# Destination rows of the message stage by a second gather, in place of a load and a 0/1 matrix

## What is computed

```python
m = x @ W_n2m.T                       # x: output of layer 0, normed
q, k, v = (m @ Wq.T + bq), (m @ Wk.T + bk), (m @ Wv.T + bv)
kj = k[src] + e                       # e from edge_attr
alpha = softmax over the edges of one dst of (q[dst] * kj).sum * scale
out = segment_sum((v[src] + e) * alpha, dst)
x_r = m @ Wskip.T + bskip
beta = sigmoid([out, x_r, out - x_r] @ Wbeta.T)
x = layernorm(x + (beta * x_r + (1 - beta) * out) @ W_m2n.T)
```

## Time and profile before

| | |
|---|---|
| median of 3 runs | 1339.7 us (1338.72 to 1341.64) |
| the profiled execution | 1339.14 us, its span 1337.4 us |
| Message, first gather to the second softmax's first transposes | 725.2 to 1107.4 us |
| steady part of it read below | 744.8 to 1080 us, 94 tiles |

### The profile page before, as it was taken

How to read it: one execution, slowest core, us unless ns; L and a number is a source line. 1 busy time by engine, 2 the same in 40 slices (tenths; PEclk the granted TensorE clock), 3 DMA queues, 4 the chain that set the end, 5 groups by cost and what they waited for, 6 DMA issues and landing times. The chain is left out here.

```text
span 1337.4 us, 29091 instructions
## 1 busy us (share of the span) xinstructions
PE 1190.2 (89%) x7386; PEld 1055.2 (79%) x7386; DVE 1042.9 (78%) x3852; ACT 813.8 (61%) x2583; POOL 839.6 (63%) x1060
## 2 busy tenths in 40 slices
PE   4999999999986899899996899999999995799990
PEld 3888999989974777777775799999999994687770
DVE  4667777777779788888885888888888877798870
ACT  1566666666657756566566566666666667376661
POOL 4888887888843645455454666666666643188885
PEclk9999999999998999999999899999999998799995
DMA  6778888888853678777786766766666632466641
GB/s 165 224 233 264 273 279 257 271 275 261 269 172 111 195 228 237 237 249 237 243 242 207 229 201 190 206 190 196 206 194 201 196 128 84 141 206 197 200 137 55
DMA packets 208940, 277.09 MB, mean 207 GB/s; under 512 B 40060, under 2 KB 140563, under 8 KB 208777
## 3 DMA queue, kind: packets, MB, share of 16 engines
q1 hardware_dynamic: 188793, 224.13, 54.3%
q0 software_dynamic: 19264, 50.85, 12.9%
q10 hardware_dynamic: 720, 0.26, 0.1%
HBM read 159.73 MB, written 117.12 MB: 207 GB/s over the span
## 5 line engine op out<-in xcount | busy, mean ns | idle before, releaser
L744 PE MATMUL banks<-m_ext,node_XT 128*128 128x257 f32 x1568 | 377.8, 384 | 0.0
L744 PEld LDWEIGHTS banks<-m_ext,node_XT 128*128 128x128 f32 x1568 | 286.6, 193 | 32.9
L671 POOL TENSOR_TENSOR node_r<-node_vv,half 128x4 f32<-128x4 f32 (+1 forms) x202 | 212.2, 1050 | 17.2 <-POOL node_vv L666 0.5
L770 DVE SCALAR_TENSOR_TENSOR node_X<-banks,node_be,node_X 128x256 f32<-128x256 f32 x392 | 169.7, 474 | 57.9 <-ACT node_be L696 56.2
L702 ACT ACTIVATE node_XT<-banks 128x512 f32<-128x512 f32 x196 | 117.1, 597 | 136.4 <-PE banks L734 129.5
L666 POOL TENSOR_SCALAR node_vv<-node_mv 128x4 f32<-128x4 f32 (+1 forms) x202 | 54.3, 269 | 202.7 <-DVE node_mv L778 182.8
L763 DVE BATCH_NORM_STATS2 node_st<-node_X 128x6 f32<-128x256 f32 x392 | 145.8, 413 | 18.5 <-DMA node_X<-in_x 17.2
L709 ACT ACTIVATE node_sq<-node_X 128x256 f32<-128x256 f32 x392 | 157.5, 406 | 0.0
L683 ACT ACTIVATE node_X<-node_X,node_r 128x256 f32<-128x256 f32 x326 | 146.0, 496 | 16.4 <-POOL node_r L671 16.4
L734 PE MATMUL banks<-ident,node_X 128*128 128x128 f32 x784 | 122.5, 279 | 29.3 <-DVE node_X L784 14.9
L824 POOL DMA_INDIRECT ring<-in_x,src_col x100 | 109.5, 1095 | 35.7 <-issue 13.8
(11 more groups left out here) (267 smaller groups left out, 2764.0 us busy)
## 6 DMA issues: line engine op xcount, KB each, us to landing
node_X<-in_x SPq DMA_DIRECT2D x196, 256.0 KB, 3.5
out<-node_X SPq DMA_DIRECT2D x196, 256.0 KB, 3.3
ring<-rows SPq DMA_DIRECT2D x210, 128.0 KB, 3.5
rows<-ring SPq DMA_DIRECT2D x100, 256.0 KB, 4.6
rows<-ring SPq DMA_DIRECT2D x200, 128.0 KB, 3.3
MB<-keeps SPq DMA_DIRECT2D x40, 320.0 KB, 5.3
store<-rows SPq DMA_DIRECT2D x90, 128.0 KB, 3.8
MB<-picks SPq DMA_DIRECT2D x50, 128.0 KB, 3.9
```

Source lines behind the costliest of these rows:

```text
L671: pool.tensor_tensor(r[:, s % 4, NT * lo:NT * hi], v, self.c.half[:, NT * lo:NT * hi], ALU.pow).then_inc(self.roots, 1)
L744: last = pe.matmul(ps[:, NT * o + k, 0:D + 1], self.XT[:, o, k * D + h * P:k * D + (h + 1) * P], c.m_ext[:, h, :], start=(h == 0), stop=(h ...
L770: last = dve.scalar_tensor_tensor(out=X[:, n % U, k, :], in0=ps[:, b + k, 0:D], scalar=self.be[:, n % 4, k:k + 1], in1=X[:, n % U, k, :], ...
```

## The change

In Message, side 0 of a ring slot is now fetched like side 1: by an indirect DMA on POOL, with the places `dst_pos` of the last edge of each edge's run. `dst_pos` comes out of the Positions part: the row of places is turned on PE and copied by ACT as integers to one column for each tile. Both sides are transposed on PE. The plain loads, the table and its loads, the comparison, the matrix product, and the gather and rewriting of the tails are gone. POOL now waits itself for the slot's earlier store (`kept`). The scratch tiles `inside` and `picked`, the tensors `tail_pos`, `lane` and `picks` are gone with them, and Output's semaphore counts are adapted.

```diff
@@ -493,23 +492,25 @@
-        self.own_sem, self.asks, self.answers, self.ready, self.table = (sem(n) for n in ("own_sem", "asks", "answers", "ready", "table"))
+        self.own_sem, self.asks, self.answers, self.ready, self.turned, self.columns = (sem(n) for n in ("own_sem", "asks", "answers", "ready", "turned", "columns"))
         def emit(s):
+            return
+        return emit
+
+    def pool(self, pool):
+        def emit(s):
+            return
+        return emit
+
+    def scalar(self, act):
+        c = self.c
+
+        def emit(s):
             if s == 3:
-                sp.wait_ge(self.ready, 1)
-                sp.dma_start(self.c.picks, self.c.scratch.picked).then_inc(self.table, 16)
-        return emit
-
-    def pool(self, pool):
-        def emit(s):
-            return
-        return emit
-
-    def scalar(self, act):
-        def emit(s):
-            return
+                act.wait_ge(self.turned, 1)
+                act.activation(c.dst_pos[:, :], c.psum[:, 7, 0:TILES], ACT.Copy).then_inc(self.columns, 1)
         return emit
...
@@ -526,6 +527,9 @@
                 pe.transpose(ps[0:TILES, 7, 256:256 + H], c.run2[:, 1, 1:TILES + 1], c.ident[0:H, 0:H]).then_inc(self.answers, 1)
+            if s == 3:
+                pe.wait_ge(self.ready, 1)
+                pe.transpose(ps[:, 7, 0:TILES], c.scratch.last, c.ident[0:TILES, 0:TILES]).then_inc(self.turned, 1)
         return emit
...
@@ -557,17 +561,13 @@
                 own(dve.tensor_copy(c.carried[:, 1, :], ps[0:TILES, 7, 256:256 + H]))
-                own(dve.memset(w.picked, -1.0))
-                own(dve.tensor_copy(c.lane[:, :], c.own_pos[:, 0:1]))
+                own(dve.memset(w.last, 1.0))
                 for k in range(2):
                 own.done()
-                own(dve.tensor_copy(c.tail_pos[:, :], w.top[:, EDGES - 1:EDGES]))
-                own(dve.tensor_scalar(w.inside, w.top, c.ends_of[:, EDGES:EDGES + 1], None, ALU.subtract))
-                own.done()
-                own(dve.scalar_tensor_tensor(out=w.picked[:, 1:1 + EDGES], in0=w.inside, scalar=float(P), in1=w.inside, op0=ALU.is_lt, op1=ALU.mult))
+                own(dve.tensor_copy(w.last[:, 1:1 + EDGES], w.top))
                 own.done()
...
@@ -874,8 +874,7 @@
                     act.wait_ge(self.masks.table, 16)
-                    act.wait_ge(self.positions.ready, 1)
-                    act.wait_ge(self.positions.table, 16)
+                    act.wait_ge(self.positions.columns, 1)
                 act.activation(c.store[:, n, 0:HP], ps[:, 6, 0:HP], ACT.Copy).then_inc(self.h_ready, 1)
...
@@ -940,6 +939,8 @@
                 n = s - 1
+                if n == 0:
+                    pe.wait_ge(self.positions.columns, 1)
                 pe.wait_ge(self.pointed, n + 1)
...
@@ -1272,12 +1270,8 @@
         self.r = sb("r", [P, 3, 4])
-        self.gathered, self.rows_in, self.kept = c.ring_in, c.ring_load, c.ring_out
-        self.in_before, self.rows_before, self.out_before = 32 * (TILES // c.R), 16 * (TILES // c.R), 32 * (TILES // c.R)
-        self.picks = [sem(f"picks{k}") for k in range(3)]
-        self.tails_in, self.tails_out, self.chosen = sem("tails_in"), sem("tails_out"), sem("chosen")
-        self.rows_v = c.rows[0:ROWS, :].rearrange("(t p) d -> t p d", p=P)
-        self.picks_v = c.picks.rearrange("(q k) m -> q (k m)", k=2)
+        self.gathered, self.kept = c.ring_in, c.ring_out
+        self.in_before, self.out_before = 32 * (TILES // c.R), 32 * (TILES // c.R)
         self.attrs = [sem(f"attrs{k}") for k in range(2)]
...
@@ -1301,12 +1295,12 @@
                     pool.wait_ge(self.finder.settled, 6)
-                    pool.wait_ge(self.positions.ready, 1)
-                    pool.indirect_dma_start(out=self.tails, out_offset=None, in_=c.rows,
-                                            in_offset=bass.IndirectOffsetOnAxis(ap=c.tail_pos[:, 0:1], axis=0)).then_inc(self.tails_in, 16)
+                    pool.wait_ge(self.positions.columns, 1)
                 at_least(pool, self.turned, n - R + 1)
-                pool.indirect_dma_start(out=c.ring[:, n % R, 1, :], out_offset=None, in_=c.rows,
-                                        in_offset=bass.IndirectOffsetOnAxis(ap=c.src_pos[:, n:n + 1], axis=0)).then_inc(self.gathered[n % R], 16)
+                pool.wait_ge(self.kept[n % R], self.out_before + 16 * (n // R))
+                for side, col in ((1, c.src_pos), (0, c.dst_pos)):
+                    pool.indirect_dma_start(out=c.ring[:, n % R, side, :], out_offset=None, in_=c.rows,
+                                            in_offset=bass.IndirectOffsetOnAxis(ap=col[:, n:n + 1], axis=0)).then_inc(self.gathered[n % R], 16)
             if t % 2 == 0 and live(t, -2, TILES):
...
@@ -1327,19 +1321,6 @@
                 sp.dma_start(self.into[n, :, :], c.ring[:, n % R, 0, :]).then_inc(self.kept[n % R], 16)
-            if live(t, -self.A, TILES):
-                n = t + self.A
-                if n == 0:
-                    sp.wait_ge(self.positions.table, 16)
-                    sp.wait_ge(self.tails_in, 16)
-                    sp.dma_start(self.rows_v[:, 0, :], self.tails).then_inc(self.tails_out, 16)
-                    sp.wait_ge(self.tails_out, 16)
-                sp.wait_ge(self.kept[n % R], self.out_before + 16 * (n // R))
-                sp.dma_start(c.ring[:, n % R, 0, :], self.rows_v[n, :, :]).then_inc(self.rows_in[n % R], 16)
-                if n % 2 == 0:
-                    at_least(sp, self.chosen, n - 4)
-                    sp.dma_start(self.picked[:, n // 2 % 3, :, :].rearrange("p k n -> p (k n)"),
-                                 self.picks_v[n // 2:n // 2 + 1, :].to_broadcast([P, 2 * P])).then_inc(self.picks[n // 2 % 3], 16)
             if t % B == 2 and live(t, -6, TILES):
...
@@ -1363,11 +1344,9 @@
                 at_least(pe, self.zt_ready, t)
-                pe.wait_ge(self.chosen, t + 1)
-                for h in range(2):
-                    pe.transpose(ps[:, 5, h * P:(h + 1) * P], c.ring[:, t % R, 1, h * P:(h + 1) * P], c.ident[:, :])
-                for h in range(2):
-                    last = pe.matmul(ps[:, 5, (2 + h) * P:(3 + h) * P], c.ring[:, t % R, 0, h * P:(h + 1) * P], self.pick[:, t % 4, :], start=True, stop=True)
+                for side in range(2):
+                    for h in range(2):
+                        last = pe.transpose(ps[:, 5, (2 * side + h) * P:(2 * side + h + 1) * P], c.ring[:, t % R, 1 - side, h * P:(h + 1) * P], c.ident[:, :])
                 last.then_inc(self.turned, 1)
...
@@ -1439,8 +1418,7 @@
                 n = t + 3
-                dve.wait_ge(self.gathered[n % R], self.in_before + 16 * (n // R + 1))
-                dve.wait_ge(self.rows_in[n % R], self.rows_before + 16 * (n // R + 1))
+                dve.wait_ge(self.gathered[n % R], self.in_before + 32 * (n // R + 1))
                 at_least(dve, self.measured, n - 1)
...
@@ -1458,11 +1436,6 @@
                 last.then_inc(self.measured, 1)
-            if live(t, -2, TILES):
-                n = t + 2
-                dve.wait_ge(self.picks[n // 2 % 3], 16 * (n // 6 + 1))
-                at_least(dve, self.turned, n - 3)
-                dve.tensor_scalar(self.pick[:, n % 4, :], self.picked[:, n // 2 % 3, n % 2, :], c.lane[:, 0:1], None, ALU.is_equal).then_inc(self.chosen, 1)
             if live(t, -1, TILES):
...
```

More of the change, by code:

```diff
@@ L152, in __init__ @@
         self.top = take(TILES, EDGES)
-        self.inside = take(TILES, EDGES)
-        self.picked = take(TILES, P)
+        self.last = take(TILES, P)
 LOADS = 16 * (1 + 4 + 6 + 3 + 1 + 3 + 5)
@@ L494, in sem @@
             return c.semaphore(nc, ctx, "positions_" + name)
-        self.own_sem, self.asks, self.answers, self.ready, self.table = (sem(n) for n in ("own_sem", "asks", "answers", "ready", "table"))
+        self.own_sem, self.asks, self.answers, self.ready, self.turned, self.columns = (sem(n) for n in ("own_sem", "asks", "answers", "ready", "turned", "columns"))
     def sync(self, sp):
         def emit(s):
-            if s == 3:
-                sp.wait_ge(self.ready, 1)
-                sp.dma_start(self.c.picks, self.c.scratch.picked).then_inc(self.table, 16)
+            return
         return emit
@@ L893, with __init__ @@
     FIRST, LAST = 0, TILES // 4 + 1
-    def __init__(self, nc, c, ctx, io):
-        self.c = c
+    def __init__(self, nc, c, ctx, io, positions):
+        self.c, self.positions = c, positions
         self.src = io["src"].rearrange("(s a e) -> s a e", a=1, e=self.B * EDGES)
@@ L1263, in __init__ @@
         self.attr_v = io["edge_attr_64"].rearrange("(q k e) a -> q e k a", k=self.B, e=EDGES)
-        self.picked = c.MB_flat[:, self.B * P:self.B * P + 6 * P].rearrange("p (a k n) -> p a k n", a=3, k=2)
-        self.pick = c.MSG_flat[:, 2 * self.B * RAD:2 * self.B * RAD + 4 * P].rearrange("p (a n) -> p a n", a=4)
-        self.tails = c.AT_flat[0:TILES, 0:D]
```

(8 more changed lines are left out.)

## The result

The changed kernel takes **1367.3 us** (median of 4 runs, 1366.2 to 1368.0); the kernel before, timed beside it, takes 1340.7 (1338.7 to 1342.7). The ratio is 1.0184, with a 95% interval from 1.0162 to 1.0206: slower. The profiled execution took 1368.0 us and its span is 1366.2, against 1339.1 and 1337.4 before.

What follows compares the result with a forecast made beforehand. PE bounds Message now at 3.57 us a tile; with the change POOL would at 3.85. The profiled 1339.1 us + 17.2 for the later softmax + 2 for waits = 1358; own range 1350 to 1366, outer 1338 to 1375.

Steps and rivals of the forecast that it cites:

- A further gather costs 1.25 us.: POOL in Message: each added gather occupies 1.25 us, gap included, raising POOL from 2.60 to 3.85 us a tile.
- The rival in which the gaps could be hidden: POOL in Message: gaps aren't work, so PE stays the bound; 1312 us, or about 1328; 9 in 100.
- PE, 0.24 us less a tile.: PE in Message: transposes replace products, saving 0.24 us a tile, to 3.32; the most the change could give.
- PE busy about 87%: Sign in the changed kernel's Message, about 745 to 1106 us: PE busy about 87% at full clock.
- 2 us for waits of POOL.: Message: allowance of 2 us in all for POOL waiting on DVE's statistics.
- The rival in which POOL waits as well: Message: gathers land late, so POOL's power waits too; up to 33 us more, 1366 to 1391; 12 in 100.
- The start.: Start of Message: six more gathers paid by a wait that goes; POOL's power at L1316 19.2 us after the first gather.
- The end, -8.9 us.: End of Message: last gather's end to second softmax shortens by 8.9 us; softmax at 1124.6, 17.2 us later than now.
- PE has drained its backlog by then: End of Message: PE has no backlog left after the last gather, which gives back 9 of the 26 us.
- The rest of the span.: Before Message's first gather and after the second softmax: no difference counted, 0 us.
- A stretched gather.: Gathers on POOL: a rule says DVE's two-port operations hold them up; no row bore it out, nothing added.
- The clock.: PE in Message: rival that idle gaps halve the clock for a tenth of the stage; 1383 us, 4 in 100.

Runs made afterwards that it cites:

- e2_more: The kernel before plus one more gather a tile on POOL, of the source rows into a place nobody reads; ratio to the kernel before 1.0162.
- e10_lean: The changed kernel with Message's addition of epsilon done by DVE instead of POOL; ratio to the kernel before 1.0002, Message 361.4 us.
- e6_plain: The changed kernel with side 0 by a plain load instead of a gather, still transposed on PE; 1317.9 us, 0.9853 of the kernel before.
- e7_nopow: The changed kernel without POOL's power in Message, rows scaled by a constant; 1320.4 us, 0.9862 of the kernel before.
- e9_after: The changed kernel itself, unchanged, measured again in another batch; ratio to the kernel before 1.0103.
- e3_nopow: The changed kernel without POOL's power in Message, rows scaled by a constant, the same edit as e7_nopow on another chip; 1.0426 of the kernel before.
- e1_plain: The changed kernel with side 0 by a plain load instead of a gather, the same edit as e6_plain on another chip; 0.9905 of the kernel before.

## Why the prediction was right, and what was off

Direction, mechanism and the outer range, 1338 to 1375, held; 1358 was 9 us too low. The forecast's own range, 1350 to 1366, was missed by 1.3 us: the measured time lies in the outer range by room that was left for rivals which didn't occur. That part was luck.

- *"A further gather costs 1.25 us."* Right. POOL's steady part ran at 3.835 us a tile against 3.85, and the 95 new gathers with their gaps (90.3 + 29.7 us) average 1.26. From the first gather to the end of the last it was 26.6 us more, for 26.1 and 2 of waits. e2_more shows the cost apart from the rest of the change, e10_lean that POOL's list sets the pace. The rival in which the gaps could be hidden is refuted for this kernel: 0.3 us stood ahead of nearly every gather while the other engines waited for POOL.
- *PE, 0.24 us less a tile.* Right in size (e6_plain: 352.3 to 331.2 us, 21.1 over 99 tiles, 0.21 a tile) and worth nothing here, as said. "PE busy about 87%" was low: 91%. Part of that is how it is shown: ahead of a stop four transposes count 0.60 us, back to back the next group starts 0.44 us after them, and the stretch has 39 stops. The rest wasn't taken apart.
- *2 us for waits of POOL.* Too much: 1.4 us of gaps ahead of L1310, none of them a wait for DVE. The rival in which POOL waits as well didn't occur. DVE did wait 29.3 us for rows, the last gathered ones, but that wait is POOL's lateness handed on, for the landing, 3.9 us in the median and at most 5.2, is as before (4.0 and 5.4).
- *The start.* Right relative to itself: 19.4 us to the power that was followed, for 19.2. The first statistics started 5.9 us after the first gather, predicted 6.5.
- *The end, -8.9 us.* Off by 2.7: it was -6.2. The step put the transposes of tile 97 at 4.9 us after the end of the last gather; DVE's norm ended 5.2 us after it, nearly as reckoned (the 0.26 us taken for it from the earlier trace rows is the comparison's, but the sum came out: 1.70 us from the last statistics to the end of that norm, for 1.8), but PE came to the tile only at 7.4. "PE has drained its backlog by then" was the false sentence: PE still had 2 us of it, and was busy for 21.18 of the last 21.30 us. From the transposes to the softmax it was 13.9 us for 13.7.
- *The rest of the span.* This is the term that was missing, put at nothing without a word, and most of the miss: +6.1 us ahead of the stage's first gather and +2.2 after the softmax. The instructions of Gather, the stage ahead, are the same in both kernels; there its last product on PE starts at 720.5 us in the changed kernel and at 715.4 and 715.5 in the two profiles of before, at 713.2 in e6_plain and at 718.4 in e7_nopow. DVE's waits for the rows of Nodes between 450 and 720 us run in nearly the same order: 16.8 us, 14.7 and 13.6, 10.2, 14.3. The four runs of the changed kernel lie within 1.8 us, so within one batch it isn't noise from run to run. But e6_plain has the changed kernel's instructions up to there and begins Message 8.4 us earlier, and e9_after, the changed kernel itself, was 7.2 us quicker from Gather's start to Message's. So these instructions alone don't bring the 6.1 us with them. Why the stretch differs by 7 us wasn't found, and it stays open whether the 8.3 us belong to the change.
- *A stretched gather.* The gathers average 1.104 and 0.950 us with DVE busy 77% of the time, and the longest of 200 took 1.252. By the Trainium skill, SBUF — State Buffer, "SBUF: two separate sides", a DMA of GpSimd is held up while DVE runs an operation in a mode with two ports. No stretch of the size that the page tells of is seen, but no row shows that any of DVE's operations here ran in that mode, so the rule is not tested.
- *The clock.* The granted clock was 0.99 in the changed kernel's steady part and 1.00 in e6_plain, which has the same transposes and a full PE. It fell to its lower level once in the middle, after PE had stood still for 2.23 us for DVE's norm (0.83 granted from 935 to 945 us), but a mean of 0.99 is far from the rival's half clock for a tenth of the stage. By the Trainium skill, TensorE: Matmul & The Clock Gate, "Part 4: PE-mode transpose", a transpose doesn't count as busy for the clock as other matmuls do; with four transposes a tile among the products, e6_plain's 1.00 shows no harm from it.

The lesson for the range: the stages that aren't changed need a spread of 5 to 8 us of their own in it.

## What to carry to other kernels

Before work is given to an engine that looks 64% busy, count what stands between its instructions: a gap that is there ahead of every gather even where the other engines wait for this one has to be counted as its work, and the room is only what is left. A saving on the engine that bounds a stage is worth only the distance to the next engine's list, so work out each list per tile before trading PE's time for GpSimd's. When the bound has moved, look for the small things on the new one (0.25 us of addition gave 17 us) and then lay the filler work of other stages anew.

## What the runs showed of the hardware

Two gathers of 128 rows of 1 KB each, one right behind the other on GpSimd, start 1.25 us apart at the closest: 0.95 us shown busy and 0.3 us not. That is the least distance in all ten profiles with two gathers a tile, and over the whole stage also in the four with one. A gather behind another kind of instruction is mostly shown with 1.10 us, and the next then starts 1.40 or 1.41 us after it (the least distance from 800 to 900 us in the four profiles with one gather a tile). An addition over 128 x 4 values that is shown with 0.25 us took 0.35 us of the stage each (17.7 us for 50). And one program's time differed by 2 to 4% between batches on different chips, while a stage bound by another engine kept its time to 0.2 us (378.9 and 379.1). In the longer batches some profiles show ACT standing still for 2 to 3 us at a time for nothing that the trace names (78 us in Message in e3_nopow, 47 in e2_more, none in e1_plain); in e3_nopow, with Message at 393.4 us for 326.1, the stage's time wasn't kept.
